# Asking for the second and third group of an adjacency mask later: after the gathered rows of the first two tiles have landed

## The reference

```python
q = neuron_states @ Wq.T          # neuron_states: layernorm of x
k = neuron_states @ Wk.T
v = neuron_states @ Wv.T
mask = adjacency.T                # 4096 x 4096, true with probability 0.000488
scores = jnp.where(mask, q @ k.T, NEG)
attn = jnp.where(mask, jax.nn.softmax(scores, axis=1), 0.0)
x = x + attn @ v
...
probs = jax.nn.softmax(layernorm(x) @ W_router, axis=-1)      # 8 experts, the best 2 of a row
out = sum over e of combine[:, e:e+1] * (relu(x @ W1[e] + b1[e]) @ W2[e] + b2[e])
x = x + out
```

## Time and profile before

| | |
|---|---|
| time, median of 3 runs | 870.7 us (870.02 to 871.3) |
| the profiled execution, its own time | 869.89 us |
| its span | 868.2 us |
| PE busy | 705.0 us (81%) |
| PEld busy | 640.5 us (74%) |
| DVE busy | 574.5 us (66%) |
| ACT busy | 455.6 us (52%) |
| POOL busy | 426.1 us (49%) |
| mean granted clock of TensorE | 0.888 of full |

### The profile page before, as it was taken

How to read it: one execution, slowest core, us unless ns; L and a number is a source line. 1 busy time by engine, 2 the same in 40 slices (tenths; PEclk the granted TensorE clock), 3 DMA queues, 4 the chain that set the end, 5 groups by cost and what they waited for, 6 DMA issues and landing times.

```text
span 868.2 us, 22858 instructions
## 1 busy us (share of the span) xinstructions
PE 705.0 (81%) x6398; PEld 640.5 (74%) x6399; DVE 574.5 (66%) x2058; ACT 455.6 (52%) x1286; POOL 426.1 (49%) x482
## 2 busy tenths in 40 slices
PE   2549999999987704461899999999999999999994
PEld 1448888888877404450798998889889899898993
DVE  8745766667866667526676866758676766766554
ACT  2636556655565303332556656556555656556563
POOL 2077777777750287775144343343334334444443
PEclk9559999999997755565899999999999999999997
DMA  9884345541211023566532231422333142122121
GB/s 291 265 214 120 86 110 143 134 124 46 79 43 49 27 84 100 162 228 226 185 109 74 95 122 56 150 79 89 115 118 107 61 158 73 51 73 62 53 64 34
DMA packets 89587, 96.73 MB, mean 111 GB/s; under 512 B 10427, under 2 KB 78533, under 8 KB 89404
## 3 DMA queue, kind: packets, MB, share of 16 engines
q1 hardware_dynamic: 70860, 61.46, 24.1%
q0 software_dynamic: 18672, 34.66, 12.5%
HBM read 82.25 MB, written 30.33 MB: 130 GB/s over the span
## 4 chain that ended last, share of the span: by engine, by line
PE 36%; issue 6%; DMA 5%; DVE 4%; POOL 2%; DVEq 1%; ACT 1%; POOLq 0%; SPq 0%; ACTq 0%
PE psE L1426 11%; PE psH L1415 6%; PE psH L1417 6%; PE psH L1416 6%; PE psE L1428 5%; DMA acc<-out,tok_next 4%; PE psX L1402 2%; POOL out L586 1%; DVE y_out L1122 1%; DMA out<-y_out,tok_now 1%; DVE h_lo L1146 1%; DVE x_lo L1100 0%; ACT x_hi L1617 0%; POOL acc L577 0%; DMA x_in<-expert_in 0%
## 5 line engine op out<-in xcount | busy, mean ns | idle before, releaser
L1631 ACT ACTIVATE z_all<-psH,b1T 128x256 f32<-128x256 f32 x296 | 142.6, 482 | 161.3 <-PE psH L1417 160.6
L1426 PE MATMUL psE<-w_parts,h_hi 128*128 128x512 f32 x552 | 209.6, 406 | 2.6 <-DVE h_lo L1146 1.9
L502 POOL DMA_INDIRECT nbr<-xn_rows,idx x160 | 165.0, 1031 | 83.7 <-issue 81.3
L1146 DVE TENSOR_TENSOR h_lo<-z_all,h_hi 128x256 fp32r<-128x256 f32 x296 | 122.7, 424 | 83.6 <-ACT h_hi L1632 82.9
L1415 PE MATMUL psH<-x_hi,w_hi 128*128 128x256 f32 (+1 forms) x592 | 166.1, 281 | 11.1 <-issue 7.6
L1417 PE MATMUL psH<-x_hi,w_lo 128*128 128x256 f32 (+1 forms) x592 | 165.8, 280 | 0.0
L1416 PE MATMUL psH<-x_lo,w_hi 128*128 128x256 f32 (+1 forms) x592 | 165.6, 280 | 0.0
L1428 PE MATMUL psE<-w_parts,h_lo 128*128 128x256 f32 x552 | 154.9, 281 | 0.0
L1632 ACT ACTIVATE h_hi<-psH,b1T 128x256 fp32r<-128x256 f32 x296 | 142.1, 480 | 0.0
L586 POOL DMA_INDIRECT out<-y_out,tok_now x74 | 77.2, 1043 | 114.3 <-DVE y_out L1122 98.2
L1415 PEld LDWEIGHTS psH<-x_hi,w_hi 128*128 128x128 f32 x592 | 112.2, 190 | 22.6 <-issue 15.0
(11 more groups left out here) (335 smaller groups left out, 1168.5 us busy)
## 6 DMA issues: line engine op xcount, KB each, us to landing
w_raw<-in_L_ffn_W SPq DMA_DIRECT2D x16, 1024.0 KB, 5.4
x_in<-expert_in SPq DMA_DIRECT2D x38, 260.0 KB
adj_even<-in_adj SPq DMA_DIRECT2D x4, 2048.0 KB
late<-in_adj SPq DMA_DIRECT2D x4, 2048.0 KB
x_all<-in_x SPq DMA_DIRECT2D x4, 1024.0 KB, 9.3
xn_rows<-z_all SPq DMA_DIRECT2D x4, 1024.0 KB
out<-x_all SPq DMA_DIRECT2D x4, 1024.0 KB, 4.9
expert_in<-pad_row SPq DMA_DIRECT2D x8, 390.0 KB, 4.8
```

The source lines that it names most:

```text
L502: pool.indirect_dma_start(nbr[:, u * K + k, :], None, xn_rows, bass.IndirectOffsetOnAxis(ap=idx[:, u, k:k + 1], axis=0), bounds_check=ROW0 ...
L1146: dve.tensor_tensor(h_lo[:, hc, :], h_f[:, hc, :], h_hi[:, hc, :].bitcast(F32), ALU.subtract).then_inc(hl_ready, 1)
L1426: pe.matmul(psE[:, q, :], h_hi[:, hc, m], w2_parts[:, b, hc].rearrange("p s c -> p (s c)"), start=(hc == 0), stop=False)
L1631: act.activation(h_f[:, hc, :], psH[:, hc % 4, 0:T], ACT.Relu, bias=b1T[:, e * HC + hc:e * HC + hc + 1])
```

## The change

SyncE gets two waits. It asks for group 1 of the adjacency only when `gathered[0]` has come to 80, that is, when the five gathers of tile 0 have landed; and it enters the loop, whose first request is that for group 2, only when `gathered[1]` has come to 80, the gathers of tile 1. Nothing else is touched.

```diff
                 sp.dma_start(adj_in[b], adj_u8[:, :, bass.ds(g * (GT * P), GT * P)]).then_inc(adj_loaded[b], 16)
+            sp.wait_ge(gathered[0], K * 16)
             next_group(1, 1)
+            sp.wait_ge(gathered[1], K * 16)
             with sp.Fori(1, NG // 2) as i:
                 next_group(i * 2, 0)
                 next_group(i * 2 + 1, 1)
```

## The result

| | before | after |
|---|---|---|
| median of 3 runs | 870.7 us (870.02 to 871.3) | 876.16 us (875.44 to 876.52) |
| ratio to before | | 1.0063 [1.0044, 1.0083] |
| profiled execution, its span | 869.89, 868.2 | 876.16, 874.5 |

The kernel became 5.5 us slower; 874.6 was forecast, 3.9 us slower.

The account below looks back on a forecast made before the run. PE's attention loop was taken as the bound, POOL close behind, so its shift reaches the end whole: + 9.65 - 4.92 - 0.8 = +3.9 us, with the base 874.6 us, 0.45% slower; range 871.2 to 877.0.

Parts of the forecast that it names:

- What bounds: Attention, 62 to 262 us: PE's loop ends last, POOL close behind; a shift of it reaches the kernel's end whole.
- When the request comes: SyncE's request for group 1: tile 0's gathers land 2.0 us after issue, moving it from 40.21 to 49.9.
- How long group 1 takes: Group 1's load: 9.9 us from request to landing, lower bound 8.0, so it lands at 59.8.
- The rival of a quick load: Group 1 takes 8.0 us with nothing asked behind it, lands at 57.9; time 872.7; chance 0.13.
- Who waits: PE at the degree of tile 4: 9.65 us later, less 4.92 idle, so weighing starts 4.7 us later.
- The clock's give-back: PE from weighing to next degree: the clock rises sooner and returns 0.8 us, bounds 0 and 2.4.
- The base: Whole kernel: 3.9 us added to the profiled 869.89 gives 873.8; 0.8 up to the median gives 874.6.
- a sign that it is wrong: PE's loop and masks: wrong if the low-clock stretches change in number.
- its rival: PE's low-clock stretches near 171, 232 and 282 to 287 us vanish: down to 868.8; chance 0.12.
- the likeliest case: Whole kernel: the forecast's own case, 874.6 us, range 872.3 to 876.4; chance 0.62.
- The second wait: Group 2, asked near 59.8, lands by 69.7; PE needs it at some 87: 17 us cover, no cost.
- POOL: Last gather in the attention 1.4 us late, landing by 258.3, ahead of the score at 262.5: no cost.

Follow-up runs that it names:

- 46 extra matmuls: Changed kernel plus 46 matmuls into an unused bank on PE, ahead of the degree of tile 4: 878.45 us, 1.0065.
- 30 extra matmuls: Changed kernel plus 30 matmuls into an unused bank on PE, ahead of the degree of tile 4: 875.29 us, 1.0045.
- Fifteen matmuls more: Second wait alone plus 11 unused matmuls ahead of the degree of tile 4 and 4 ahead of tile 0's weighing: 883.69 us, 1.0152.
- 26 more: Second wait alone plus 18 unused matmuls ahead of the degree of tile 4 and 8 ahead of tile 0's weighing: 872.0 us, 1.0003.

## Why the prediction was right, and where its size was off

*What bounds.* Right. A shift of PE's loop reached the first scatter and the experts. Group 1 behind the query of tile 1 used the 4.92 us to spare and cost nothing, group 1 behind tile 1 cost 6.6 us for 6.97 more.

*When the request comes.* The gathers landed 1.5 us behind their last issue, not 2.0, so the request stands at 49.30 instead of 49.9.

*How long group 1 takes.* Predicted 9.9, measured 10.25, and 9.8 to 10.9 in the other kernels, with or without group 2 on the queue behind it. The rival of a quick load (8.0) is out. The fit of the Trainium skill, DMA: Bandwidth & Descriptors, section Anatomy of one DMA, which is for transfers that GpSimd asks for and gives an estimate of 6.8 us for these bytes, was not reached by any of these transfers of SyncE.

*Who waits.* PE's first degree on group 1 came 9.40 us later (59.55 against 50.15), so 9.40 - 4.92 = 4.5 was to come by these numbers; measured 4.34 at the weighing (predicted 4.7).

*The clock's give-back: mis-sized.* The step was "I take 0.8, a third". From weighing to the degree of tile 5 it took 6.31 us against 6.50 before: 0.19 came back. The clock rose only at the end of the weighing, in the window of 65 to 66 us (0.60, from 0.50 before it). The 2.2 to 2.4 us at stake are real, as the 46 extra matmuls show, but how much comes back differs where the order of the rows is the same: 0.2 in the repeat of the changed kernel, 0.9 with the first wait alone and with group 1 behind tile 1, 1.0 with it behind tile 1's query. The 0.8 lies among these, and no run shows what decides between them. At tile 5 the error here is 0.6, and the weighing's 0.36 in the other direction takes more than half of it back: 4.15 in place of 3.9.

*The base.* The profile of before that the sum was made against has two low-clock steps. The changed kernel has three between the degrees of tiles 5 and 31, and so have eight of the other profiles, among them three of kernels that leave group 1's request at its place, and the one behind tile 1's query. Of before there is one profile; its 869.89 us lie 1.9 under the median of before in the later runs (871.75). The prediction named a change in the number of these steps as a sign that it is wrong, and this sign came; its rival had only the other direction, that they vanish. It is one more: + 1.65 us by tile 31. At the masks the clock gave 1.18 back. Against the kernel behind tile 1's query, which costs nothing and has three such steps as well, the changed kernel is 4.99 us late at tile 5 (0.85 of it from the clock, which rose sooner there: from weighing to degree 5.46 us against 6.31) and 4.98 at tile 31: the shift passes the loop whole. Its median is 4.5 us above that one, and 4.7 above that of before in the repeat. So the 5.5 us of the first comparison holds the mechanism's 4 to 4.7 us, and the rest lies within the intervals of the two ratios.

*Luck.* The prediction's own terms end at 875.4, and 876.16 lies above that. It falls into the likeliest case's 872.3 to 876.4 only by what was allowed for scatter. The shift at tile 5, 4.15 us, lies within the terms' bounds of 0.4 to 4.7; the low-clock step and the experts' stage, which carried the profile to 6.3, stand in no term.

*The second wait.* "Costs nothing" was right in the changed kernel, but the step missed that it is worth something alone. I had it as cover for group 2, and credited the earlier landing of tile 0 to the first wait. Taking group 2 away is enough for that: 50.75, against 49.39 with both groups held back. That earlier start is what the rows show behind the 3 us by which the second wait alone is under the median of before beside it (868.75 and 871.75).

*POOL.* The verdict "no cost" was right, its working wrong. The last gather starts at 258.37, 4.5 us later than in the earlier trace rows, not 1.5, as POOL gets its row numbers and free buffers from a loop that is itself late. From tile 7 on each tile's first gather starts 1.1 to 2.0 us behind the row that makes its numbers, where it was 2.7 to 6.3 before: POOL's spare time is gone, and it follows the loop. The last score waits 2.13 us for `q_sb`, about as before, so POOL did not become the bound.

*Not traced:* the 1.7 us of the experts' stage, above.

## What to carry to other kernels

Before a transfer is held back to clear the way for another, look at what stands behind the wait for it on the in-order engine, and read off that engine's idle time right behind it: that much delay is free, and beyond it the slope was near one here. Of two transfers that load the same queues, hold back the one that is needed last; here the second wait alone made the kernel 3 us faster, and with the first it was about 5 us slower. And where a gain is a few microseconds of an engine that has idled, expect its clock to take it: compare durations of the same row, and count the low-clock steps in more than one profile before a sum is made against one of them.

## What the runs showed of the hardware

- In a loop in which PE is busy for 92% of the time, single steps of 6.65 us took 8.31. In the changed kernel these came 61.5 us apart (74.22, 135.72, 197.22); in the second wait alone at 100.84, 168.99 and 230.49. No run shows what sets their place.
- The column of the granted clock can lag behind. In the repeat of the changed kernel the window below reads 1.00, while the weighing that began at 62.08 took 4.62 us, as at half clock. The durations decide.

```profile
62.00:66.00 4.00, 4.00 (x27) 4.00 (x24) 2.65 (x13) 0.89 (x2) 3.08 (x4) 1.00 1.06 291
```

- The clock can fall while PE is busy and has paused for little: with 30 extra matmuls PE idled 0.59 us after 15 us of work, and was at 0.50 from 62 us on.
- Fifteen matmuls more, ahead of a loop, brought PE two standstills of 2.6 and 2.9 us and two of 2.9 and 3.2 within the loop, with instruction loads beside them; 26 more, at the same places, brought none. Loads on the same queue from 78 to 118 us brought none in either, so a load by itself is not enough.
